# ScalarE's order within a gather group of a graph network's edge passes: exponent or absolute difference first, then the matrix items

## The reference

```python
# layer 0 (difference pass)
h_src = h[src]
edge_feats = jnp.abs(h[dst] - h_src)
seg_sum = segment_sum(concat([h_src, edge_feats]) @ W_edge.T + b_edge, dst)
# layer 1, twice (attention passes), with a loop edge at each node
att = jnp.einsum('ehd,ehd->eh', q[dst], k[src]) / scale      # 8 heads of 16
att = jnp.clip(att, -50.0, 50.0)
ex = jnp.exp(att - m[dst])
alpha = ex / (segment_sum(ex, dst) + 1e-16)
aggr = segment_sum(v[src] * alpha, dst)
```

## Time and profile before

| | us |
|---|---|
| median of three runs | 8621.14 (8603.41 to 8645.64) |
| profiled execution | 8688.01 |
| its span | 8686.2 |
| PE busy | 6259.8 (72%) |
| VectorE busy | 4877.5 (56%) |
| ScalarE busy | 3177.4 (37%) |
| GpSimd busy | 2478.4 (29%) |
| mean granted clock of PE | 0.85 of 2.4 GHz |

### The profile page before, as it was taken

One profiled execution on the slowest core, in us unless ns is written; L12 is line 12 of the kernel. 1 busy time (PEld: TensorE's weight loads), 2 busy tenths in 40 slices (PEclk: granted clock), 3 DMA queues, 4 the chain that ended last, 5 costly groups with the idle time before them and its releaser, 6 DMA issues. The chain is left out here.

```text
span 8686.2 us, 132811 instructions
## 1 busy us (share of the span) xinstructions
PE 6259.8 (72%) x30617; PEld 4137.9 (48%) x30618; DVE 4877.5 (56%) x14511; ACT 3177.4 (37%) x6207; POOL 2478.4 (29%) x2517
## 2 busy tenths in 40 slices
PE   7997998477777754565566665566656669999988
PEld 3443444366555544444444454444444444444433
DVE  9999888566666635666666655666666651100000
ACT  2552554255555522344444442344444430000000
POOL 0000000266555600455555510555555500000000
PEclk9999999689988876777777777777777779999999
DMA  0000000144444420444445521444444507777799
GB/s 15 0 0 0 0 0 15 55 137 137 135 135 136 136 48 28 141 157 152 156 156 160 161 60 33 139 145 145 146 142 147 145 17 283 289 273 287 288 374 397
DMA packets 445515, 1166.14 MB, mean 134 GB/s; under 512 B 93566, under 2 KB 156606, under 8 KB 413148
## 3 DMA queue, kind: packets, MB, share of 16 engines
q1 hardware_dynamic: 336652, 891.04, 27.5%
q0 software_dynamic: 106496, 272.79, 12.5%
q10 hardware_dynamic: 2256, 0.89, 0.0%
HBM read 759.01 MB, written 404.15 MB: 134 GB/s over the span
## 5 line engine op out<-in xcount | busy, mean ns | idle before, releaser
L665 POOL DMA_INDIRECT ACC<-tab_kv,STAGE x1664 | 1621.6, 974 | 2251.3 <-DMA STAGE<-IDX 814.4
L1173 ACT ACTIVATE PS<-PS,X 128x512 f32<-128x512 f32 x1456 | 967.9, 665 | 1476.9 <-remote 891.0
L870 PE MATMUL PS<-ITEM 128*128 128x512 f16 x1456 | 672.6, 462 | 898.1 <-ACT PS L1173 671.7
L732 PE MATMUL PS<-Q 128*128 128x416 f16 x6464 | 1174.7, 340 | 93.5 <-DVE Q L1445 93.5
L1640 DVE TENSOR_TENSOR ACC<-ACC,PS 128x137 f32 (+1 forms) x2288 | 749.9, 328 | 799.0 <-remote 390.3
L858 PE MATMUL PS<-SCR 128*128 128x137 f32 x3328 | 668.9, 359 | 541.2 <-DVE ACC L1640 378.2
L665 POOL DMA_INDIRECT SCR<-tab_h,STAGE x832 | 847.0, 1018 | 731.3 <-PE PS L862 271.7
L732 PEld LDWEIGHTS PS<-Q 128*128 128x128 f16 x6464 | 611.5, 98 | 656.7 <-issue 197.8
L858 PEld LDWEIGHTS PS<-SCR 128*128 128x128 f32 x3328 | 563.1, 246 | 722.6 <-DVE ACC L1640 500.7
L840 PE MATMUL PS<-Q,SCR 128*128 x4992 | 846.1, 323 | 83.6 <-issue 71.0
L840 PEld LDWEIGHTS PS<-Q,SCR 128*128 128x128 f32 x4992 | 780.1, 231 | 224.6 <-issue 202.3
(11 more groups left out here) (291 smaller groups left out, 8056.9 us busy)
## 6 DMA issues: line engine op xcount, KB each, us to landing
ACC<-adj SPq DMA_DIRECT2D x252, 1792.0 KB, 6.8
adj<-X SPq DMA_DIRECT2D x936, 256.0 KB
adj<-ITEM SPq DMA_DIRECT2D x520, 256.0 KB
ACC<-tab_kv,STAGE POOLq DMA_INDIRECT x1664
SCR<-tab_h,STAGE POOLq DMA_INDIRECT x832
tab_kv<-SCR SPq DMA_DIRECT2D x14, 896.0 KB, 4.1
ACC<-adj SPq DMA_DIRECT2D x21, 448.0 KB, 4.2
tab_h<-SCR SPq DMA_DIRECT2D x7, 448.0 KB, 3.0
```

Source lines behind the costliest of these rows:

```text
L665: nc.gpsimd.indirect_dma_start(G[:, q, j, 0:w], None, table, bass.IndirectOffsetOnAxis(STAGE[:, u, q * S4 + j:q * S4 + j + 1], 0))\
L732: ins = nc.tensor.matmul(SUMS[:, at:at + w], OHP[:, u, k, :], OHS[:, u, q * w:(q + 1) * w], start=first and u == 0, stop=last and u == RIN ...
L870: nc.tensor.matmul(CLASS_SUM[k % 2], OHS1[:, k % ring, :], OHD[:, k % ring, :], start=False, stop=True, skip_group_check=True).then_inc(ad ...
L1173: nc.scalar.activation(CLASS_SUM[(k + 1) % 2], CLASS_SUM[k % 2], ACT.Copy, scale=KEEP[:, bass.ds(i, 1)])\
```

## The change

In ScalarE's `body` of an edge pass, the call for the group's first item moves from before the exponent or absolute difference to after it, where the other items of the group already stand. No instruction is added or removed, and the lines behind it move up by one (L1189 becomes L1188, L1192 becomes L1191).

```diff
                     own = items_of(name, it, u)
                     if exists(gi + 2):
                         copy(it if u < 2 else it + 1, (u + 2) % 4)
-                    item(it, *own[0])
                     wait(act, s, "att", gi + 1)
                     if kind == "att":
                         wait(act, s, "agg", gi - 1)
...
                     else:
                         nc.scalar.activation(M[:, u % 2, :, 0:D], PROD[:, :, :], ACT.Abs).then_inc(s["msg"], 1)
-                    for each in own[1:]:
+                    for each in own:
                         item(it, *each)
```

## The result

The changed kernel took 8646.06 us (median of 20 runs, 8630.69 to 8656.33) against 8628.62 us for the kernel before. The ratio is 1.002 with a 95% interval of 1.0011 to 1.0028: slower by 17 us, where 145 us less were forecast, and just inside the range's upper end of 8,650.

A forecast was written before the change was run, and what follows sets the result against it. Waits between engines, not a full engine, were taken to bound the edge passes. 145 us from attention and nothing from the difference pass gave 8,688 - 145 = 8,543, scaled to the runs' median as 8,477 us; range 8,350 to 8,650.

The forecast's parts named there:

- The loop S, clip, X, M, S: Attention passes: a loop of waits between PE, VectorE and ScalarE sets the time, and a late X lengthens it.
- S: PE's summing matmuls of a group (L858, or L860 and L862 in the difference pass).
- X: ScalarE's exponent in an attention group (L1189 before the change).
- M: VectorE's multiply that makes the messages in an attention group (L1693 before the change).
- X starts 1.05 us earlier and M's wait falls: Attention passes: X starts where the first item's work started, removing 246 of VectorE's 281 us of waiting before M.
- What reaches S: Attention passes: hidden at full clock; at half clock the item's matmul delays S, so 34 us come off, leaving 212.
- X's own wait: ScalarE, attention: X must now wait for the clip; costed at nothing, 83 us at most.
- the item's matmul in front of S: PE: it now needs an item copy made after X; 0.25 us to spare at full clock, not hidden at half clock.
- What is swallowed: Attention: M's gain is lost where VectorE's next group's first multiply waits for PE's expansion, 31%; 212 becomes 146, taken as 145 us.
- The rival "swallowed": VectorE's wait before M reappears before L1678 and L1640; about 30 us of gain left, 8,590 us; chance 0.20.
- The difference pass costs nothing: Difference pass: a tenth of a microsecond won at full clock and lost at half; between 21 us gain and 31 us loss.
- the two rivals: PE's clock in attention: rises to 0.80, 8,400 us, chance 0.12; or idle PE lowers it to 0.62, 8,675 us, chance 0.12.

The follow-up runs named there:

- e16: The whole change against the kernel before, on a chip of the faster kind: 7555.83 against 7727.41 us, ratio 0.978.
- e2: First item moved behind the exponent in the attention passes only, against the kernel before, faster kind of chip: 7583.74 against 7728.83 us, ratio 0.981.
- e17: Kernel before plus one unused 0.69 us VectorE instruction per attention group, faster kind of chip: 7907.79 against 7727.41 us, ratio 1.024.
- e14: Kernel before plus two unused VectorE instructions per attention group, faster kind of chip: 8146.85 against 7715.11 us, ratio 1.056.
- e10: Kernel before plus one unused 0.69 us VectorE instruction per attention group, slower kind of chip: 8581.41 against 8687.85 us, ratio 0.988.
- e5: The changed kernel run again, against the kernel before, slower kind of chip: 8635.18 against 8620.35 us, ratio 1.0018.
- e8: The changed kernel run once more, against the kernel before, slower kind of chip: 8718.99 against 8687.85 us, ratio 1.0032.
- e9: First item moved behind the exponent in the attention passes only, against the kernel before, slower kind of chip: 8724.68 us, ratio 1.0037.
- e1: The kernel before, unedited, profiled a second time, on a chip of the faster kind: 7,725 us.
- e7: Changed kernel plus six unused matmuls before each attention group's summing, against the kernel before, slower kind of chip: 8635.47 us, ratio 1.0019.
- e11: Changed kernel plus six unused matmuls before each attention group's summing, another set, against the kernel before, slower kind of chip: 8727.90 us, ratio 1.0043.
- e6: Kernel before plus six unused matmuls before each attention group's summing, slower kind of chip: 8731.31 us, ratio 1.0133 against the kernel before.

## Why the prediction was wrong, point by point

**The loop S, clip, X, M, S.** Right for chip B: there the change gives 172 us, the attention part 145 us (e16, e2), and added work in the loop costs time (e17, e14). For the chip of the result it is not what sets the time (e10).

**X starts 1.05 us earlier and M's wait falls.** Right in kind on both. From the end of the clip to X it took 1.79 us in the mean before and 1.00 after in att0, 1.45 and 0.67 in att1: some 0.8 us earlier and not 1.05. M's wait fell from 281 to 94 us on chip A, short of the "under 80" that was said, and in att0 of chip B from 143.9 to 33.9. The sum of the smaller of wait and 1.05 us was put at 246 us; counted again in the trace of before it is 224 with the waits over 0.15 us and 237 with all. With it the forecast gain would have been 131 to 140 us instead of 145.

**What reaches S; X's own wait; the item's matmul in front of S.** Right for chip B: PE's wait before the item's matmul grew by 133 us in att0 and the pass became shorter all the same. On the chip of the result a sign of being wrong came true: from M to S it took 1.39 us before and over 1.7 us in none of the 416 groups, after it over 1.7 us in 71 of the 208 groups of att0 (66 in e5); the median of every second group there is 1.87. The item's matmul is late there, as was feared for the half clock:

```profile
3574.81 2.07 PE L840 MATMUL PS<-Q,SCR 128*128 x8 [0.18 <-issue]
...
3575.13 0.69 DVE L1692 TENSOR_TENSOR SCR<-ACC,SCR 128x512 f32<-128x512 f32 x1
...
3576.68 0.63 PE L870 MATMUL PS<-ITEM 128*128 128x512 f16 x1
...
3577.10 2.03 PE L858 MATMUL PS<-SCR 128*128 128x137 f32 x8
```

Over 1.39 us these groups lose 41 us in all, close to the 34 taken off for it. It doesn't decide the result: e8 has 8 such groups, e9 12, and their loss against the kernel before is the larger one.

**What is swallowed: 31%, this is the step that failed.** I took for it the groups in which L1678 waits for something "remote", 128 of 416, and let the rest go by: with the label "issue" L1678 waits in 215 more, and before the sums (L1640) there are 210 waits, which I left out since S "does move" with M. Of the 212 us that were to reach S the prediction let 66 be swallowed. On chip A all of it was, and 17 us more: of the 187 us that VectorE no longer waits before M, 178 turn up before L1678 and L1640. The sign of it stood in the rows: "remote" ended 137.0 + 176.8 us of waits in the earlier trace rows and 3.17 us in the earlier trace rows, and I treated it as a wait for PE's work, which would be done earlier with the rest of the loop. In the place above the work was done and the signals were held for five microseconds. How much of the 178 us is of this kind isn't shown, as a share of the records is missing. The rival "swallowed" named L1678 and L1640 as the places and was the nearest, but at 8,590 us it still kept 30 us of gain.

**The difference pass costs nothing, bounds 21 us of gain to 31 of loss.** On chip B the gain is 25 us, twice, a little past the bound. In the one pair of traces on chip A the pass is 17 us shorter.

**The clock.** Neither of the two rivals: 0.75 and 0.75 before, 0.76 and 0.74 after.

**Agreement that is partly luck.** e2's 145.1 us equal the forecast 145, but chip B's waits before M were shorter (209 us in e1, not 281) and a larger part of what went arrived in the time.

**Open.** What makes PE's signals late in spells on chip A and not on chip B, whether the recording has a part in it, why only in the edge passes, and why VectorE waits less when it has more to do. e10 suggests that the spells depend on how the engines stand to each other, e7 that they don't need the low clock. The edit's small loss on chip A (0.2 to 0.4%, in four comparisons) is of this kind, and I have only this argument for it: that the spells come out a little worse in the new order is not shown by a run of its own.

## What to carry to other kernels

Before a wait is priced, look at what ended the waits beside it: a large "remote" share before several engines at once, released within a tenth of a microsecond, can mean that the signals are late and not the work, and then a shorter loop of work need not give a shorter time. The times of the semaphore updates decide it: several in less time than the work between them takes. And add up an engine's waits by the instruction behind them, over all labels and pass by pass, before saying where a wait went. Lengthening the suspected loop by one instruction whose result isn't used is the cheapest test of whether it sets the time; here it cost 2.4% on one chip and won 1.2% on the other. And a change should be judged on more than one chip, where that can be had: this one is 2.2% faster on one and 0.2% slower on the other.

## What the runs showed of the hardware

- The same program took 8,620 to 8,690 us on some chips and 7,715 to 7,729 us on others, 10 to 11% less, with sorting and dense stages equal and all of the difference in the gather passes.
- On the slower ones signals of PE's matmuls came in late spells: in the place shown four of them within 0.19 us, the first 4.8 us after its modelled end (e1, on one of the others: ScalarE starts 0.12 us after the end in the row shown, and there is no "remote" among the leading waits).
- The traces of the slower ones lack a part of the semaphore updates in the edge passes and none in the sorting and dense stages (in the attention passes of before 39% of VectorE's and ScalarE's, 17% of PE's; in e1 under 1%).
- 287 us of extra VectorE work made the kernel 106 us faster on the one and 180 us slower on the other.
- Six extra matmuls in each attention group raised the mean granted clock of the first attention pass from 0.75 to 0.86; they cost 0 to 9 us in the changed kernel and 111 us in the kernel before (e7, e11, e6).
